# Zero rows up to 96 under the operands of six groups of small matmuls, in a two-layer attention and mixture-of-experts kernel on one Trainium2 core

## What is computed

```
x = x + attention0(layernorm(x), ctx, mask)
# layer 0 experts: E=16, I=96, sigmoid router, top 4 in the top 2 of 4 groups
combine = (tokens x 16), four weights per token, scaled by 2.5
h = silu(x @ w1) * (x @ w3) * combine            # per expert
x = x + h @ w2 + shared_expert(x)
x = x + attention1(layernorm(x), ctx)
# layer 1 experts: E=8, H=256, softmax router, top 2
combine = (tokens x 8)
y = gelu(layernorm(x @ w1 + b1)) @ w2 + b2       # per expert
x = layernorm(sum_e combine * y + x)
```

## Time and profile before

| | |
|---|---|
| median of three runs | 260.47 us (258.6, 260.47, 260.87) |
| the profiled execution | 259.6 us, of which the span of its instructions is 257.8 us |
| busy share of the span | PE 89%, PE weight loads 53%, DVE 72%, ACT 60%, POOL 30% |
| granted TensorE clock, mean | 0.994 of full speed (2.4 GHz) |
| experts of layer 0, 97 to 144 us | PE busy 44.12 us of 47.00, DVE 31.56, ACT 13.66, POOL 3.32 |
| attention of layer 1, 144 to 196 us | PE busy 48.41 us of 52.00, DVE 43.42, ACT 36.63 |
| its last heads and the experts of layer 1, 196 to 258 us | PE busy 50.05 us of 62.00, DVE 43.27, ACT 38.08 |

### The profile page before, as it was taken

How to read it: one execution, slowest core, us unless ns; L and a number is a source line. 1 busy time by engine, 2 the same in 40 slices (tenths; PEclk the granted TensorE clock), 3 DMA queues, 4 the chain that set the end, 5 groups by cost and what they waited for, 6 DMA issues and landing times.

```text
span 257.8 us, 5097 instructions
## 1 busy us (share of the span) xinstructions
PE 229.2 (89%) x1656; PEld 136.4 (53%) x1656; DVE 186.8 (72%) x578; ACT 155.5 (60%) x225; POOL 77.8 (30%) x223
## 2 busy tenths in 40 slices
PE   2879899999999999999899779999988989989871
PEld 1553444445444547868676444454444447767660
DVE  7678786776676384677755897888865657789864
ACT  6675896666964762341232467777775674696570
POOL 4581442465522100100200241444422042344321
PEclk9999999999999999999999999999999999999997
DMA  6768799920110038700033492400000000000000
GB/s 204 255 203 167 195 154 165 320 79 18 47 61 3 3 66 154 148 2 0 0 113 73 130 356 80 112 4 0 4 0 3 0 0 4 1 0 3 0 20 22
DMA packets 18180, 20.41 MB, mean 79 GB/s; under 512 B 1553, under 2 KB 15609, under 8 KB 17825
## 3 DMA queue, kind: packets, MB, share of 16 engines
q1 hardware_dynamic: 17578, 19.16, 29.4%
q10 hardware_dynamic: 576, 0.94, 1.2%
HBM read 15.90 MB, written 4.19 MB: 78 GB/s over the span
## 4 chain that ended last, share of the span: by engine, by line
PE 58%; DVE 22%; issue 8%; DMA 4%; ACT 3%; POOL 2%; SPq 1%; DVEq 1%; POOLq 0%; ACTq 0%
PE bank L372 11%; PE bank L447 9%; PE bank L425 8%; PE bank L421 5%; DVE st L1056 4%; PE bank L545 4%; PE bank L565 4%; PE bank L546 3%; DVE row_max L871 3%; PE bank L620 2%; PE bank L378 2%; ACT q_stack L1364 2%; DVE shared_area L1094 1%; DMA aw<-in_attn_w 1%; DMA k_bounce<-early 1%
## 5 line engine op out<-in xcount | busy, mean ns | idle before, releaser
L1379 ACT ACTIVATE probs<-bank 128x1024 f32<-128x1024 f32 x64 | 64.3, 1023 | 14.1 <-PE bank L425 9.0
L868 DVE CUSTOM_DVE_ANT_0 discard<-bank,bias_q 128x512 bf16<-128x512 f32 x64 | 43.3, 690 | 17.5 <-PE bank L372 16.1
L372 PE MATMUL bank<-k_stack,q_stack 72*128 72x512 bf16 x128 | 48.4, 384 | 4.5 <-DVE row_max L871 1.8
L871 DVE TENSOR_REDUCE row_max<-bank 128x1 f32<-128x512 f32 x64 | 42.0, 687 | 9.4 <-PE bank L372 5.8
L425 PE MATMUL bank<-q_stack,k_stack 102*128 102x256 bf16 x256 | 43.7, 272 | 0.2 <-ACT q_stack L1364 0.2
L447 PE MATMUL bank<-probs,v_ext 128*32 128x256 f32 x512 | 40.3, 391 | 0.2 <-ACT o_sb L1386 0.2
L1364 ACT COPY q_stack<-bank 6x512 bf16<-6x512 bf16 x32 | 18.5, 578 | 27.7 <-PE bank L394 27.6
L425 PEld LDWEIGHTS bank<-q_stack,k_stack 102*128 102x128 bf16 x256 | 24.8, 98 | 17.1 <-issue 1.4
L1620 POOL CAST max_part<-row_max 128x4 bf16<-128x4 f32 x32 | 6.3, 195 | 81.3 <-DVE row_max L871 45.2
L372 PEld LDWEIGHTS bank<-k_stack,q_stack 72*128 72x128 bf16 x128 | 12.2, 96 | 27.8 <-issue 12.6
L421 PE MATMUL bank<-bias_k,idb 128*128 128x512 bf16 x64 | 24.3, 380 | 0.3 <-ACT q_stack L1364 0.2
(11 more groups left out here) (187 smaller groups left out, 360.4 us busy)
## 6 DMA issues: line engine op xcount, KB each, us to landing
k_stack<-k_bounce SPq DMA_DIRECT2D x9, 384.0 KB
q_bounce<-q_part SPq DMA_DIRECT2D x12, 192.0 KB, 2.9
k_bounce<-early SPq DMA_DIRECT2D x4, 384.0 KB, 3.3
experts_w<-in_wu SPq DMA_DIRECT2D x1, 1024.0 KB, 4.9
early<-in_wu SPq DMA_DIRECT2D x1, 1024.0 KB, 7.1
experts_w<-in_wg SPq DMA_DIRECT2D x1, 816.0 KB, 14.1
experts_w<-in_wu SPq DMA_DIRECT2D x1, 816.0 KB, 16.4
experts_w<-in_wd SPq DMA_DIRECT2D x1, 768.0 KB, 16.9
```

The source lines that it names most:

```text
L372: mm(bank[:, qt, :], q_stack[0:STACK, b, h, qt * 128:(qt + 1) * 128], k_stack[0:STACK, b, h, :], start=True, stop=True).then_inc(for_max, 1)
L868: ins = dve.tensor_tensor_reduce(discard[:, qt, :], bank[:, qt, :], bias_q[:, qt, :], 1.0, LOWEST, ALU.add, ALU.max, o)
L871: ins = dve.tensor_reduce(o, bank[:, qt, :], AX.X, ALU.max)
L1379: act.activation(probs[:, n % (2 * HG), :], bank[:, at:at + 2, :].rearrange("p a n -> p (a n)"), ACT.Exp, scale=SCALE).then_inc(exp_done, 1)
```

## The change

A constant `WIDE = 96` becomes the number of rows, or of weight columns, of the operands named above. `sel`, `c_rows`, `cT1` and `bd1_sb` have 96 partitions in place of 48 or 8; `c_part` and the layer 1 combine weights have 96 columns per token tile, of which the old 48 or 8 are used. The rest is zero: POOL clears `sel`, `c_part`, `bd1_sb` and the two `combine1` tiles once, after group 5 of the maxima. The copies to `c_rows` and `cT1` take 96 partitions. Three waits on the clearing are added: DVE before its first use of `c_part`, ACT before the cast into `sel`, SP before the load of `bd1_sb`.

```
+WIDE = 96
-        bd1_sb = sb("bd1_sb", [E1, D])
+        bd1_sb = sb("bd1_sb", [WIDE, D])
-        sel = sb("sel", [PARTS * E0, T0, 128], BF16)
+        sel = sb("sel", [WIDE, T0, 128], BF16)
-        combine = [[sb(f"combine{l}{b}", [128, QT, (E0, E1)[l]]) for b in range(B)] for l in range(2)]
-        c_part = sb("c_part", [128, QT, PARTS, E0], BF16)
+        combine_wide = [sb(f"combine1{b}", [128, QT, WIDE]) for b in range(B)]
+        combine = [[sb(f"combine0{b}", [128, QT, E0]) for b in range(B)], [c[:, :, 0:E1] for c in combine_wide]]
+        c_part_wide = sb("c_part", [128, QT, WIDE], BF16)
+        c_part = c_part_wide[:, :, 0:PARTS * E0].rearrange("p t (a e) -> p t a e", a=PARTS)
-        c_rows = [sb(f"c_rows{b}", [PARTS * E0, S], BF16) for b in range(B)]
-        cT1 = [sb(f"cT1{b}", [E1, S]) for b in range(B)]
+        c_rows = [sb(f"c_rows{b}", [WIDE, S], BF16) for b in range(B)]
+        cT1 = [sb(f"cT1{b}", [WIDE, S]) for b in range(B)]
...
-                        o = bank[0:PARTS * E0, 1 if first else MISC, 0:128].bitcast(BF16)
-                        last = pe.transpose(o[:, t * 128:(t + 1) * 128], c_part[:, t].rearrange("p a e -> p (a e)"), idb[:, :])
+                        o = bank[0:WIDE, 1 if first else MISC, 0:128].bitcast(BF16)
+                        last = pe.transpose(o[:, t * 128:(t + 1) * 128], c_part_wide[:, t, :], idb[:, :])
                     else:
-                        last = pe.transpose(bank[0:E1, MISC, t * 128:(t + 1) * 128], combine[1][b][:, t, :], idf[:, :])
+                        last = pe.transpose(bank[0:WIDE, MISC, t * 128:(t + 1) * 128], combine_wide[b][:, t, :], idf[:, :])
...
                     if b == 0:
+                        dve.wait_ge(pads_zeroed, 3 + B)
...
-                    then(copy(c_rows[b][:, :], bank[0:PARTS * E0, 1 if first else MISC, 0:128].bitcast(BF16)))
+                    then(copy(c_rows[b][:, :], bank[0:WIDE, 1 if first else MISC, 0:128].bitcast(BF16)))
                 else:
-                    then(copy(cT1[b][:, :], bank[0:E1, MISC, 0:S]))
+                    then(copy(cT1[b][:, :], bank[0:WIDE, MISC, 0:S]))
...
                 act.wait_ge(ld["sel"], 16)
-                act.copy(sel[:, :, :], sel_f[:, :, :]).then_inc(sel_ready, 1)
+                act.wait_ge(pads_zeroed, 3 + B)
+                act.copy(sel[0:PARTS * E0, :, :], sel_f[:, :, :]).then_inc(sel_ready, 1)
...
+            def zero_pads():
+
+                pool.memset(sel[:, :, :], 0.0).then_inc(pads_zeroed, 1)
+                pool.memset(c_part_wide[:, :, :], 0.0).then_inc(pads_zeroed, 1)
+                pool.memset(bd1_sb[:, :], 0.0).then_inc(pads_zeroed, 1)
+                for b in range(B):
+                    pool.memset(combine_wide[b][:, :, :], 0.0).then_inc(pads_zeroed, 1)
...
                 (4, lambda: v_bias(1)),
+                (5, lambda: zero_pads()),
                 (6, lambda: add_row(0, 0, "bo0")),
...
+            sp.wait_ge(pads_zeroed, 3 + B)
+            sp.dma_start(bd1_sb[0:E1, :], bd1).then_inc(ld["wd1"], 16)
```

More of the change, by code:

```diff
@@ L212, in attention_ffn_kernel @@
         sel_ready = sem("sel_ready")
+        pads_zeroed = sem("pads_zeroed")
         wu1_ready = sem("wu1_ready")
@@ L1782, in _ @@
             sp.dma_start(wsd0_sb[:, :], wsd0).then_inc(ld["wd0"], 16)
-            sp.dma_start(bd1_sb[:, :], bd1).then_inc(ld["wd1"], 16)
+            sp.wait_ge(pads_zeroed, 3 + B)
+            sp.dma_start(bd1_sb[0:E1, :], bd1).then_inc(ld["wd1"], 16)
             k_out(2)
```

## The result

The changed kernel took 256.25 us, the median of four runs (255.99 to 256.88); the kernel before, with a fourth run added to the three, 259.54 us (258.19 to 260.87). The ratio is 0.988, with a 95% interval of 0.984 to 0.992. It is faster, by 1.2%; the forecast was 258.1 us. The profiled execution took 256.07 us, its span 254.2 us.

A forecast was written before the change was run, and what follows sets the result against it. PE was taken as the bound (58% of the chain of waits). Layer 0 experts 2.18 plus layer 1 0.28 less copies 0.08 made 2.4 us: 259.6 became 257.2, with 0.9 to the median 258.1 us, range 256.5 to 260.2.

The forecast's parts named there:

- The base: End step: the profiled execution's 259.6 us gives 257.2; it lies 0.9 under the runs' median, 260.47, hence 258.1 us.
- the sum: Saving on PE that reaches the end of the kernel: 2.18 + 0.28 - 0.08 = 2.4 us.
- Experts of layer 0: Transposes and spread pairs on PE, walked from wait to wait: 0.50 + 1.48 + 0.20 = 2.18 us saved.
- The tail: Layer 1 bias products on PE: 0.16 us saved for the first sequence, 0.12 for the second, 0.28 together.
- The wider copies: Second c_rows copy and second cT1 copy, both on the path: up to 0.04 us more each, 0.08 against the gain.
- The lost savings: Layer 0 experts: five spread pairs and one group of transposes gain nothing at the end; about 1.1 us.
- A: Everything comes through: the groups counted as lost gain too, 3.5 us saved, 257.0 us; chance 0.08.
- B: Less comes through: PE's saving turns into waits for DVE, or weight-loading time stays; 258.9 or 259.3 us; chance 0.21.
- the second cost: On PE behind a spread: first matmuls recorded 0.11 us longer (0.70 against 0.59), their weights not loaded ahead.
- C: DVE is held during POOL's clearings: PE loses up to 1.8 us at 41 to 44, 259.9 us; chance 0.06.
- D: Slower than before: POOL's clearings take 5.3 us and hold DVE all that time, 262.6 us; chance 0.04.
- E: A size of 96 is not treated as full size: nothing gained, 260.5 us; chance 0.05.

The follow-up runs named there:

- e6: Changed kernel with 96 rows in the spread alone, transposes and bias product as before: 257.12 us, ratio 0.9915 to the kernel before.
- e3: The changed kernel again, unaltered: 256.53 us, ratio 0.9897 to the kernel before.
- e11: The changed kernel once more, unaltered, beside its variants: 256.84 us, ratio 0.9904 to the kernel before.
- e9: Changed kernel with operands of 72 rows in place of 96, run once: 256.25 us.
- e7: Changed kernel with the spread reading the old 48 rows, transposes and bias product still at 96: 258.32 us, ratio 0.9966 to the kernel before.
- e8: Changed kernel with the largest clearing, of `sel`, done three times more ahead of the rest: 257.69 us, ratio 0.993 to the kernel before.
- e2: Changed kernel with 64 rows or columns in place of 96: 259.36 us, ratio 1.002 to the kernel before.
- e4: Changed kernel with attention's value products issued for two key tiles together throughout: 256.79 us, ratio 0.9914 to the kernel before.
- e10: Changed kernel with value products of all four key tiles together in layer 0's first three groups of heads: 257.87 us, ratio 0.9958 to the kernel before.
- e12: Changed kernel with value products two key tiles at a time in layer 0's first three groups, run again: 254.99 us, ratio 0.9857 to the kernel before.
- e5: Changed kernel with value products two key tiles at a time only in layer 0's first three groups: 256.39 us, ratio 0.9882 to the kernel before.

## Why the prediction was right and wrong

**The step that failed is the last one:** "it lies 0.9 under the median of the runs, 260.47, and against that the time is 258.1". The base was wrong, not the gain. The median of three runs was taken for the kernel's time. A fourth run moved that median by 0.93 us, to 259.54, and 66 later runs of the same kernel have a median of 259.32 us; only 7 of them lie above 260.47. They fall into two kinds, by the mean granted clock that stands with each run: 52 runs at over 0.9925 took 258.11 to 259.72 us, median 259.1; 14 at 0.992 and less took 260.02 to 261.2. e6 shows what such a lower mean can be made of: one stretch at half clock, 1.65 us. Two of the three runs shown, 260.47 and 260.87, are as long as the second kind; their clocks are not on record. The measured gain, 2.56 us, taken from 259.1 gives 256.5; the changed kernel's 17 runs (with e3, e11 and e9's of 72 rows) have a median of 256.42, and none has a clock under 0.993. Of the 1.85 us between the forecast and the result, the base makes 1.37, the sum 0.16, and 0.32 is left to the spread of four runs. The other base that the prediction had, the profiled execution, was nearer but high as well: its first score row, at 19.95 us, is among the latest of the fourteen profiles. The lower end of the range took off 0.5 us for the base where it was off by 1.4; the spread of the three runs (2.3 us) was counted among the chances of slower and belonged there too.

**The sum held:** 2.4 us forecast, 2.56 measured between the profiled executions from the first score row on.
- Experts of layer 0: 2.18 forecast; 0.12 + 2.07 = 2.19 measured, of which the transposes of `c_part` 0.26 (e7; 0.25 forecast) and the spreads 1.93 (e6; 2.18 less 0.25). The 0.12 lies ahead of the transposes' own start, where the stop on going in was.
- The tail: 0.28 forecast for the bias products; 0.34 measured (0.33 in e7), so the fill behind them was not slower, as I had allowed.
- The wider copies: 0.08 forecast against it, nothing measurable. The copies to `cT` took 8 ns longer (388 for 380), on 96 partitions in place of 8; the 0.04 came from another copy, L889's.
- The lost savings: "about 1.1 us" forecast, 0.94 more idle time measured. At the second place of the earlier trace rows the wait did not grow but fell from 0.51 to 0.19 us, since PE now stands idle for 0.37 us ahead of the first score rows of layer 1, at 133.82. That is a wait which the walk did not have: it took the DMAs to start earlier together with the rest, and these transfers did not. They hang on the query projection, L347, which from the first score row on came 1.4 us earlier (108.47 to 107.08), and the three spreads behind it shortened only PE's way. So the first score rows of layer 1 came 1.7 us earlier, and not 2.2 as the prediction said. By the last wait for DVE the whole 2.19 us was there: the wait for row maxima is 0.32 us shorter, and one more spread follows.

**The rivals.** A, that everything comes through, would have given 257.0, close to what was measured, but for a wrong reason: the idle times show 0.94 us lost. B fails: the gain is still there 68.7 us further on, and the L549 pair behind a spread lasts 0.59 us, so the second cost went too. C and D fail: DVE's operation takes 0.69 us beside clearings, in the changed kernel and in e8, where they last three times as long. E fails for 96 and for 72 rows, and would have been right for 64 (e2).

**Where the line runs.** Weights of 64 rows (and of 64 columns, in the transposes) cost what 48 did, 72 cost nothing. The Trainium skill (TensorEngine Tiling (Array Packing), "Key Properties") says that a change of the tiling mode drains the TensorE, and its "Overview" calls a contracted or a free dimension of up to 64 small. The stops of this case fit that, on a kernel that asks for no tiling: one costs 0.09 to 0.10 us, and 64 is on the small side and 72 is not. That the small products are put in such a mode is an inference; the trace shows the stops and not the mode. Size alone does not decide: the f32 transposes into 8 columns have no stop toward L585 (0.22 us for two), while bf16 transposes into 48 and 64 columns do. No run here varied the type of a transpose, so what tells them apart is not shown. They stand on the large side: eight records of value products ahead of them take 0.57 us to the next start (205.06 to 205.63 before), as they do ahead of a score row.

**What stays open.** Why the changed kernel had no run of the slower kind in 17, when before had 14 in 66, is not explained; at equal odds that happens about once in 60 times. Its variants e4 to e8, e10 and e12 have such runs. Nor does any run separate the f32 transposes, which pay no stop, from the rest.

## What to carry to other kernels

Read TensorE by the distance from start to start and compare the same form with and without a small product beside it: a stop of 0.1 us on each side, too short for any idle time to be shown, was worth 2.5 us here over some 30 matmuls, and zeros up to 72 rows were enough. Look at each kind of product before padding it: the f32 transposes had no stop to lose. Count a saving only up to the next wait for another engine; that walk gave 2.18 where 2.19 was measured, though it overlooked a DMA on the way. Work put off into a larger burst saves stops, but first ask whether it now fills a time in which the engine waits. And before a gain of 1% is set against a median of three runs, look at how far those three lie apart: here the base was off by half as much as the change was worth.

## What the runs showed of the hardware

- PE stops by 0.09 to 0.10 us between a matmul of 8, 48 or 64 rows and one of 72 or more, either way (of 8 rows only the way out was seen), and so it does with the bf16 transposes into 48 or 64 columns. The weights of the matmul behind such a change begin to load with the matmul itself, where they otherwise load 0.11 us ahead (107.38 before, 105.53 for 105.64 after); an f32 pair behind a spread lasts 0.11 us longer (0.70 for 0.59). Value products of 32 columns do it too: six groups fewer gave 1.2 us (e5, e12). The f32 transposes into 8 columns do not (0.22 us for two, up to the next matmul).
- The granted clock fell to half for 3.4 us in the middle of some executions (e6, from 151.1; e4, from about 190), with PE busy for 7.12 of the 9.00 us ahead and no idle time there over 0.46 us. It cost 1.65 us in e6.
- The time of the first score row ranged from 18.77 to 20.10 us over the profiles, while the first weights arrived at 4.32 to 4.69 and PE waited up to 1.24 us (e7) for `q_stack`. That range is half of the gain.
- A matmul that waited for a DMA started 0.08 to 0.10 us behind its last landing, in five profiles. Three of them (the changed kernel's, e3, e11) show the wait as idle time without a releaser, the other two (e6, e9) show no idle time at all.
- Beside POOL's clearings a DVE operation with one operand in PSUM and one in SBUF kept its 0.69 us.
